# A GRU scan with experts on one core: order of the start's transfers, bias products made once, spare products, and the place of GpSimd's work

## What is computed

```python
def cell(h, x):
    gi = x @ W_ih + b_ih
    gh = h @ W_hh + b_hh
    r = sigmoid(i_r + h_r); z = sigmoid(i_z + h_z)
    n = tanh(i_n + r * h_n)
    return (1 - z) * n + z * h
# for all states h of the scan:
logits = h / max(norm(h), 1e-12) @ router_w      # softmax, the top 2, renormalised
out = x + sum_e combine[:, e] * (h @ Wa[e] @ Wb[e])
```

## Time and profile before

| | |
|---|---|
| median of 3 runs | 1004.74 us (1004.66 to 1004.81) |
| the profiled execution | 1004.69 us |
| its span in the trace | 1002.9 us |
| PE busy | 968.7 us, 97% |
| DVE busy | 881.9 us, 88% |
| ACT busy | 692.6 us, 69% |
| POOL busy | 290.7 us, 29% |
| granted clock of PE, mean | 0.999 |

### The profile page before, as it was taken

How to read it: one execution, slowest core, us unless ns; L and a number is a source line. 1 busy time by engine, 2 the same in 40 slices (tenths; PEclk the granted TensorE clock), 3 DMA queues, 4 the chain that set the end, 5 groups by cost and what they waited for, 6 DMA issues and landing times.

```text
span 1002.9 us, 60804 instructions
## 1 busy us (share of the span) xinstructions
PE 968.7 (97%) x28971; PEld 673.8 (67%) x21187; DVE 881.9 (88%) x3653; ACT 692.6 (69%) x2697; POOL 290.7 (29%) x756
## 2 busy tenths in 40 slices
PE   4689999999999999999999999999999999999997
PEld 2456767677767677767677667777667767667764
DVE  5999888888888888888888888888888888888887
ACT  6776667766766676676676676676677677666664
POOL 1032333232323232223232223232233232233232
PEclk9999999999999999999999999999999999999999
DMA  8600111111111111111011111111111111110001
GB/s 298 176 22 19 30 33 30 28 30 32 29 32 33 25 30 34 27 33 33 25 30 36 26 32 32 26 30 36 27 33 30 28 30 33 30 31 20 14 8 30
DMA packets 50512, 39.10 MB, mean 39 GB/s; under 512 B 35684, under 2 KB 40124, under 8 KB 50236
## 3 DMA queue, kind: packets, MB, share of 16 engines
q1 hardware_dynamic: 49388, 31.67, 12.1%
q10 hardware_dynamic: 848, 3.54, 1.1%
HBM read 18.94 MB, written 8.39 MB: 27 GB/s over the span
## 4 chain that ended last, share of the span: by engine, by line
PE 88%; DVE 7%; ACT 2%; DMA 1%; issue 1%; ACTq 0%; DVEq 0%; POOL 0%; POOLq 0%
PE pairs L923 17%; PE ybank L923 11%; PE gates L1003 11%; PE gates L1008 10%; PE pairs L914 6%; PE ybank L914 5%; PE zbank L923 5%; PE zbank L914 5%; PE tbank L923 3%; PE obank L923 3%; PE nbank L923 3%; PE tbank L914 2%; PE obank L914 2%; PE nbank L914 2%; DMA wih<-in_L_cond_W_ih 1%; DVE tr L779 1%
## 5 line engine op out<-in xcount | busy, mean ns | idle before, releaser
L923 PE MATMUL pairs<-wx,xs 128*32 128x384 f16 x4464 | 296.3, 327 | 0.4 <-DVE wx L759 0.4
L643 ACT ACTIVATE rr<-pre 128x64 f32<-128x64 f32 x256 | 65.7, 257 | 235.5 <-DVE pre L782 235.3
L923 PEld LDWEIGHTS pairs<-wx,xs 128*32 128x32 f16 x4464 | 118.5, 97 | 113.0 <-issue 77.2
L923 PE MATMUL ybank<-hparts,wa 128*128 128x128 f16 x2016 | 185.2, 219 | 0.0
L914 PE MATMUL ybank<-hparts,wa 128*128 128x128 f16 x1008 | 173.8, 219 | 0.0
L923 PEld LDWEIGHTS ybank<-hparts,wa 128*128 128x128 f16 x2016 | 156.8, 98 | 23.4 <-issue 10.5
L1003 PE MATMUL gates<-whh,st 128*32 128x256 f16 x4080 | 157.1, 273 | 14.8 <-DVE st L808 14.4
L1008 PE MATMUL gates<-whh,hparts 128*32 128x256 f16 x4080 | 157.3, 273 | 0.0
L1003 PEld LDWEIGHTS gates<-whh,st 128*32 128x32 f16 x4080 | 105.2, 96 | 62.0 <-ACT gates L615 34.2
L923 PE MATMUL zbank<-whh,hparts 128*32 128x128 f16 x4080 | 145.5, 219 | 0.0
L914 PE MATMUL zbank<-whh,hparts 128*32 128x128 f16 x4080 | 145.5, 219 | 0.0
(11 more groups left out here) (153 smaller groups left out, 1891.6 us busy)
## 6 DMA issues: line engine op xcount, KB each, us to landing
out<-outb SPq DMA_DIRECT2D x63, 128.0 KB
xin<-in_x SPq DMA_DIRECT2D x60, 128.0 KB
wih<-in_L_cond_W_ih ACTq DMA_DIRECT2D x4, 768.0 KB, 7.5
whh<-in_L_cond_W_hh SPq DMA_DIRECT2D x4, 768.0 KB, 12.0
wih<-in_L_ffn_Wb SPq DMA_DIRECT2D x8, 256.0 KB, 5.2
xs<-xh SPq DMA_TRANSPOSE x120, 3.2
wih<-in_L_ffn_Wa SPq DMA_DIRECT2D x4, 256.0 KB, 6.0
whh<-in_L_ffn_Wa SPq DMA_DIRECT2D x4, 256.0 KB, 4.5
```

What stands on the lines that cost most here:

```text
L643: nc.scalar.activation(rr[:, :], pre[:, RG, :, :].rearrange("p k b -> p (k b)"), ACT.Sigmoid, scale=1 / PROD_SCALE).then_inc(r_ready, 1)
L923: return nc.tensor.matmul(out, lhsT, rhs, start=start, stop=stop, skip_group_check=True)
```

## The change

- SP's queue gets W_ih 0 and 1, `cond`, W_ih 2 and 3, W_hh 0, x block 0, W_hh 1 to 3, x block 1, the router's weights; x block 2 goes between the first loads of the experts' weights. ACT's queue gets the biases only.
- The bias products go into the first bank of `pairs` only; the second is begun with zero products, and ACT copies the first into it (`keep_biases`).
- `turn_first(1)` moves behind step 0 on PE, its high part to step 0 on ACT and its low part to step 1 on DVE; `split_x(FIRST)` on ACT moves from step 0 to step 1. In ACT's and DVE's lists before step 0, block 0, the kept biases and the seeds change their places.
- 16 spare products stand on PE ahead of block 0, 4 behind step 0. Their results aren't used.
- POOL: in steps up to 17 (`QUIET`) its work of a step, except norm, logits, gaps and `combine`, waits for the gate products of the next step. In all steps `gaps` comes before `low_y`, and both `less_upper_half` stand at s = 1.
- `LOW_AT` moves late pieces of DVE between steps.

```diff
+    QUIET = 2 * S + 1
-    LOW_AT = {1: 3, 2: 2, 3: 3, 4: 3, 5: 2, 6: 3, 7: 2, 8: 2, 9: 2, 10: 2, 11: 2, 12: 1, 14: 2, 15: 2, 17: 2}
+    LOW_AT = {1: 1, 2: 2, 3: 3, 4: 3, 5: 2, 6: 3, 7: 2, 8: 2, 9: 3, 10: 2, 11: 1, 12: 2, 13: 1, 14: 2, 15: 2, 17: 2}
+    WARM = 16
+    FILL = 4
...
+            load_ih(0)
+            load_ih(1)
+            load_cond()
+            load_ih(2)
+            load_ih(3)
+            load_hh(0)
+            load_first(0)
+            for k in range(1, K):
                 load_hh(k)
+            load_first(1)
             sp.dma_start(rw32[:, :, :], router_w.rearrange("(p k) e -> p k e", k=K)).then_inc(rw_loaded, 16)
-            sp.wait_ge(whh_loaded[1], 16)
-            load_first(1)
-            sp.wait_ge(whh_loaded[2], 16)
-            for half in range(2):
-                load_x(FIRST, half)
             sp.wait_ge(weights_split, splits_before(N_IH_SPLITS))
             for i in range(LEAD):
                 load_late(i)
+                if i < 2:
+                    load_x(FIRST, i)
...
             def beside(n):
                 i, s = n // S, n % S
+                if s == 3 and 1 <= i:
+                    invert_norm(i - 1)
+                    sum_logits(i - 1)
+                    gaps(i - 1)
+                if s == 4 and 1 <= i:
+                    combine(i - 1)
+
+                if n <= QUIET:
+                    pool.wait_ge(rh_done, n + 2)
                 if s == 0 and 1 <= i:
                     fold_squares(i - 1)
                     add_squares(i - 1)
-                if s in (1, 2) and 1 <= i:
-                    less_upper_half(i - 1, s - 1)
-                if s == 3 and 1 <= i:
-                    invert_norm(i - 1)
-                    sum_logits(i - 1)
-                if s == 4 and 1 <= i:
-                    combine(i - 1)
+                if s == 1 and 1 <= i:
+                    for part in range(2):
+                        less_upper_half(i - 1, part)
                 if s in (5, 6) and i + 2 < NB:
                     split_x(i + 2, s - 5, n)
                 for m in reads_at(n):
                     low_y(m)
-                if s == 3 and 1 <= i:
-                    gaps(i - 1)
...
             def keep_biases():
                 act.wait_ge(bias_done, 1)
-                nc.scalar.activation(bias_sums[:, :], pairs[1][:, P:4 * P], ACT.Copy).then_inc(bias_kept, 1)
+                nc.scalar.activation(bias_sums[:, :], pairs[0][:, P:4 * P], ACT.Copy).then_inc(bias_kept, 1)
+                nc.scalar.activation(pairs[1][:, :], pairs[0][:, :], ACT.Copy).then_inc(bias_kept, 1)
...
             for n in range(N_GRU_SPLITS):
                 split_weights(n)
-                if n == 8:
-                    split_first(0)
-                if n == N_IH_SPLITS:
+                if n == N_IH_SPLITS - 1:
                     keep_biases()
+                if n == N_IH_SPLITS + 2:
                     copy_high(-1)
                     act.wait_ge(consts_ready, N_CONST)
-                if n == N_IH_SPLITS + 3:
+                    split_first(0)
+                if n == N_IH_SPLITS + 8:
                     seed(0)
                     seed_z(0)
-            split_first(1)
...
+            def spare_products(count):
+                for _ in range(count):
+                    nc.tensor.matmul(nbank[:, 0:3 * P], wx[:, 0, 0, 0, 0:P], wx[:, 0, 0, 0, :], start=True, stop=True,
                                      skip_group_check=True)
...
+            put_first_biases()
+            pe.wait_ge(hi_split, 3)
+            spare_products(WARM)
             pe.wait_ge(ident_step, 2)
             turn_first(0)
-            put_first_biases()
             wait_turned(0)
             for k in range(K):
                 first_parts(k)
             pair_part(1, range(6))
-            turn_first(1)
             first_state_part()
             grouped_step(0)
+            spare_products(FILL)
+            turn_first(1)
```

More of the change, by code:

```diff
@@ L491, in less_upper_half @@
                 if f < NB - 1:
-                    pool.wait_ge(both_parts_ready, 2 * ((f + 1) * S + 3 + part))
+                    pool.wait_ge(both_parts_ready, 2 * ((f + 1) * S + 3))
                 nc.gpsimd.tensor_tensor(sqs[:, part + 1, :], sqs[:, part, :], upper_half(part), ALU.subtract
@@ L583, in _, with load_biases @@
         def _(act):
-            for k in range(K):
-                if k == 2:
-                    act.dma_start(xin[:, 0, :], x_blocks[0]).then_inc(first_loaded[0], 16)
-                act.dma_start(wih32[:, k, :, :].rearrange("p g n -> p (g n)"), W_ih[k * P:(k + 1) * P, :]
-                              ).then_inc(wih_loaded[k], 16)
+            groups = "(g j c) -> j g c"
+            def load_biases():
+                act.wait_ge(consts_ready, 2)
+                act.dma_start(bias_h[0:P:32, HN, :], b_hh[2 * D:3 * D].rearrange("(j c) -> j c", j=K)).then_inc(bias_loaded, 16)
+                act.dma_start(bias_h[0:P:32, RG:ZG + 1, :], b_hh[0:2 * D].rearrange(groups, g=2, j=K)).then_inc(bias_loaded, 16)
+                act.dma_start(bias_i[0:P:32, :, :], b_ih.rearrange(groups, g=3, j=K)).then_inc(bias_loaded, 16)
             def split_weights(n):
@@ L711, in beside @@
                 if n == 0:
+                    split_first(1)
+                if n == 1:
                     split_x(FIRST)
@@ L898, in _ @@
                 if n == 8:
+                    turn_state()
+                if n == N_IH_SPLITS + 2:
+                    low_state()
                     split_first(0)
-                if n == 8:
-                    turn_state()
-                if n == N_IH_SPLITS:
-                    low_state()
             turn_n(0, 0)
@@ L961, in put_first_biases @@
                 pe.wait_ge(bias_loaded, 16 * 3)
-                for bank in pairs:
-                    nc.tensor.matmul(bank[:, 0:4 * P], spread_rows[:, :],
-                                     bias_h[:, :, :].rearrange("p g c -> p (g c)"), start=True, stop=False,
+                nc.tensor.matmul(pairs[0][:, 0:4 * P], spread_rows[:, :], bias_h[:, :, :].rearrange("p g c -> p (g c)"),
+                                 start=True, stop=False, skip_group_check=True)
+                nc.tensor.matmul(pairs[0][:, P:4 * P], spread_rows[:, :], bias_i[:, :, :].rearrange("p g c -> p (g c)"),
+                                 start=False, stop=True, skip_group_check=True).then_inc(bias_done, 1)
+            def spare_products(count):
+                for _ in range(count):
+                    nc.tensor.matmul(nbank[:, 0:3 * P], wx[:, 0, 0, 0, 0:P], wx[:, 0, 0, 0, :], start=True, stop=True,
                                      skip_group_check=True)
-                    mm = nc.tensor.matmul(bank[:, P:4 * P], spread_rows[:, :],
-                                          bias_i[:, :, :].rearrange("p g c -> p (g c)"), start=False, stop=True,
-                                          skip_group_check=True)
-                mm.then_inc(bias_done, 1)
             def first_parts(k):
@@ L1149, in _ @@
             zeros = st[:, :, :].rearrange("p k c -> p (k c)")
-            for g, n_cols in ((gates, 2), (zbank, 1)):
+            for g, n_cols in ((gates, 2), (zbank, 1), (pairs[1], 4)):
                 for c in range(n_cols):
```

27 lines of the change are left out of this document (14 added, 13 removed).

## The result

The changed kernel takes 1008.72 us (median of seven executions), against 1004.97 for the kernel before on the same chips (1004.66 to 1005.73): ratio 1.0035, 95% interval 1.0022 to 1.0047. One of the seven took 1668.69 us at a granted clock of 0.558 and counts as disturbed; the other six lie at 1007.95 to 1009.23, with 1008.59 as their median. The kernel is slower by 3.6 to 3.8 us. The profiled execution took 1007.95 us, 3.3 more than before's 1004.69, and is the fastest of the six, so its trace shows the start of a good execution and not of a typical one.

A forecast was written before the change was run, and what follows sets the result against it. PE, busy throughout, and a loop of dependent operations with 0.1 us of slack per step were taken to bound the kernel. 1004.74 - 2.3 (start) + 1.0 (steps 1 to 17) + 4.5 (s = 3) = 1007.9 us; own range 1005.3 to 1010.2.

The forecast's parts named there:

- s = 3: Every eighth step: `gaps` first puts POOL's two y's among the loop's last DVE operations; 0.15 per period, +4.5 us.
- The start: Up to step 0: W_ih first on SP's queue brings DVE's last split to 23.6 from 25.9 us; -2.3 us.
- the landing of the last W_hh: In the start: weights at 419 GB/s and block 0 at 1.4 us put it at 20.1 to 20.9 us.
- Close to the path but not on it: In the start: block 0 lands at about 15.5, is split by 17.5 and multiplied by 19.6, when the seeds are next.
- Spare products cost nothing: On PE: 16 stand before block 0 lands, where PE idles; four behind step 0 cost 0, at most 0.4.
- Steps 1 to 17: Late splits and the gate on rh_done together: +1.0 us, range -1.5 to +2.
- the late pieces: DVE's splits moved between steps: step 9 +0.06, steps 12 and 13 +0.33 each, step 11 -0.09; sum +0.6.
- the gate: Steps up to 17: waiting on rh_done moves POOL's meetings with DVE onto L782; 2.8 us for 2.4 now.
- The folds: POOL's two folds, 0.74 and 0.46, cost the chain about 0.42, at steps 8 and 16.
- A: Rival: the y's miss the loop at s = 3; 1003.4 us (10%), or 1000.9 if the gate frees DVE (12%).
- B: Rival: the start gains nothing, the rest as forecast; 1010.2 to 1010.5 us, 8%.
- C: Rival: only the start's gain comes, steps 1 to 17 and the eighth steps unchanged; 1002.4 us, 10%.

The follow-up runs named there:

- the edit alone: The kernel before with only `gaps` moved ahead of `low_y` at s = 3: 1010.23 us, ratio 1.0055.
- the meeting taken away: The changed kernel with `gaps` put back behind `low_y` at s = 3: 1003.65 us, ratio 0.9988.
- the y's behind the next state: The changed kernel, `gaps` still first, with the two y's of s = 3 moved to the next step behind its low half: 1003.72 us, ratio 0.9982.
- the replanned kernel: The kernel with `gaps` behind `low_y`, plus two early splits on ACT, late pieces spread anew, gate ending at step 15, router's weights ahead of block 1: 1002.96 us.

## Why the prediction was right, and where it wasn't

Forecast 1007.9, measured 1008.72; the sign and the main mechanism held. Term by term, against the profile:

- **s = 3, forecast +4.5 (range 0 to 6): +5.14, and +5.3 by the edit alone.** The reading was right in place and kind: y's behind the picks, in the loop, two late operations, 30 times. It came as the variant that the prediction names: L799 (`npre`) slips in first, the first y falls on L802 (`v`), whose delay the wait for tanh hides, and the second on L804 (`u`), which is paid. 0.17 per period instead of 0.15. The page SBUF — State Buffer of the Trainium skill (Who interferes with whom) has the holder keep the shared pair for its whole instruction; `v` and `u` ending 0.14 and 0.09 us behind the two y's agree with it. The forecast by that page, 30 x 0.17 = 5.1, had the right size by luck: it was for a y ahead of L799, which didn't happen.
- **The start, forecast -2.3 (range -3.3 to -0.5): -1.61 in the profile.** In the other kernels with this start state 0 came at 26.73 to 27.32 us where the clock stayed full, -1.8 to -1.2, and at 27.72 to 28.00 where it fell. The median of the changed kernel seems to hold both kinds: three of its executions have a mean granted clock of 0.999 or 1.000 and take 1007.95 to 1008.46 us, three have 0.997 or 0.998 and take 1008.72 to 1009.23. So the start brought less there than in the profile. The term that was mis-sized is the landing of the last W_hh: forecast at 20.1 to 20.9 us, it comes at 21.72, by the trace's record of landings, 0.46 later than in the kernel before (21.26). I let weights flow at 419 GB/s throughout and block 0 cost 1.4 us. The stretches show

```profile
9.00:12.00 3.00, 3.00 (x7) 1.14 (x6) 2.93 (x6) 2.52 (x5) 0.00 (x0) 1.00 1.02 418
12.00:15.00 3.00, 3.00 (x15) 1.59 (x13) 2.74 (x6) 3.00 (x7) 1.08 (x2) 1.00 1.06 257
15.00:18.00 3.00, 0.93 (x6) 0.42 (x4) 1.87 (x4) 1.30 (x4) 0.00 (x0) 1.00 1.00 381
```

  257 GB/s where block 0 is among them and 381 behind it. By the landings, W_hh 0 to W_hh 1, with block 0 between, takes 4.23 us (13.45 to 17.68) where W_hh 2 alone takes 1.89: block 0 costs about 2.3, the difference, and not 1.4. DVE's wait before block 0 is 1.13 us where I had allowed 1.2 for all gaps together; three of 0.26 to 0.28, one before each part of W_hh that it had to wait for, come on top. And ACT, which has the seeds from 21.17 to 21.86 ahead of the last W_hh, starts on it at 21.78, so the seeds and the landing hold it up to the same moment. From there to DVE's last split it is 2.55 us, as forecast (0.6 + 1.90). The page DMA: Bandwidth & Descriptors of the Trainium skill (Specifications) has about 358 GB/s as the limit for one core; it was exceeded here too (418 and 381), so the row was the better guide. No run has the new order of transfers and nothing else.
- **"Close to the path but not on it", of block 0: on it at full clock already, by the seeds, and plainly when the clock is low.** Where the first pair's products ran at half rate, the seeds waited for them, and ACT's split of the last W_hh for the seeds: ACT started on it 0.5 us after its landing with POOL's order as before, 1.8 us without spare products, and state 0 came at 27.7 to 28.9 instead of 26.9. The prediction had no term for the clock.
- **"Spare products cost nothing": true, but that was half of it.** I costed what they take and never asked what would be lost without them. Taken out, they cost 2.0 us of start in the profiles (0.8 us by the ratios, whose intervals overlap); without them this start brought nothing in its profile (28.90 against 28.51). So what the start gained hangs on them, for a reason that the forecast didn't name. That the clock's level causes it is read from the durations at either level, not shown by a run in which only the clock changed.
- **Steps 1 to 17, forecast +1.0: +0.78, by the wrong split.** I gave +0.6 to the late pieces and +0.4 to the gate. The late pieces alone make +0.79; the new order of POOL, gate and all, makes nothing in the sum. In the trial of the pieces alone steps 12 and 13 take +0.34 and +0.25, as forecast (+0.33 each), but step 9 takes +0.50 where I had +0.06, since the third piece lies beside POOL's work, and step 11 gives 0.30 back where I had 0.09. With the gate, step 9 is +0.33, near the 0.06 + 0.25 of the forecast. The folds cost step 16 0.38, as the "about 0.42" had it. L802 was to be lengthened to 0.4 in steps 6, 7, 9 and 17; it takes 0.42 to 0.67 in steps 5, 8, 9, 10, 16 and 17, and 0.26 and 0.22 in steps 6 and 7. Two of these meetings, at steps 5 and 8:

```profile
46.72 0.45 DVE L799 STREAM_TRANSPOSE tr<-gates 128x256 f32<-128x256 f32 x1
47.20 0.67 DVE L802 TENSOR_TENSOR pre<-tr 128x64 f32<-128x64 f32 x1
...
58.67 0.42 DVE L802 TENSOR_TENSOR pre<-tr 128x64 f32<-128x64 f32 x1
```

  L802 is lengthened as foreseen, at step 8 by 0.2. At step 5 it is lengthened by 0.44 where I gave xh 0.16, because POOL didn't begin with the transpose:

```profile
47.12 0.67 POOL L485 TENSOR_TENSOR xh<-x,xh 128x256 f16<-128x256 f32 x1 [33.67 <-PE gates L1028]
50.85 0.68 POOL L485 TENSOR_TENSOR xh<-x,xh 128x256 f16<-128x256 f32 x1 [3.06 <-PE gates L1028]
```

  The first starts 0.40 behind the transpose, which waits for the same products. At step 6, the second starts 0.03 ahead of the transpose (at 50.88). Step 5 therefore gained nothing (4.09 against 4.05), step 6 0.46 (3.73 against 4.19).
- **At nothing:** the bias products, zero products, ACT's extra copy, the four spare products and the turning of block 1 behind step 0: state 0 to 1 takes 3.64 us, before 3.65. The SP queue's wait: no sign of it. Both held, also `less_upper_half` at s = 1, as far as the steps show.
- **Not forecast:** -0.91 at s = 6, and +0.21 in the tail, which I had called unchanged (last section).

Sum: -1.6 + 0.8 + 5.1 - 0.9 - 0.2 + 0.2 = +3.4, forecast +3.2. Part of that nearness is luck: the start brought 0.7 less than forecast and the loop cost 0.6 more, and 1.1 that wasn't forecast came back in other steps. By the medians the difference is 3.6 to 3.8. Of the rivals, A had the right price for the rest: with the meeting taken away the kernel takes 1003.65, forecast 1003.4. B fell in the profile (-1.61), C by the 30 steps at s = 3.

## What to carry to other kernels

Where a loop of dependent small operations sets the rate, an engine that is idle 70% of the time isn't free to use: ask of each of its operations in which part of the loop it will now lie, and whether an operation there is lengthened by it and has no wait to hide that in; moving two operations of 0.43 us to about 2 us later in the step cost 0.5% of the run. Cost a spare or warming instruction from both sides, what it takes and what would be lost without it, and look at a matmul's duration, not only at busy columns. When work is moved between steps, add up each step's free place (here 0.86 us) before and after; the three steps that got pieces too many (9, 12 and 13) grew by 1.1 us together, and planning the list by the measured prices brought 0.7 us.

## What the runs showed of the hardware that was not expected

- PE's granted clock can fall again in the start, after 7 to 10 us at the full one: to 0.50 (1.2 GHz) in five of the thirteen profiles (for example from 19.5 to 22.9 us with POOL's order as before, and from 18.2 to 21.6 with the y's behind the next state). Two of the five are of kernels with before's start. PE has idle times of 1.5 us and more between its bursts there, and the same instructions kept 1.00 in other profiles. In the three profiles of a new start in which it fell, PE was idle for 1.5 to 2.2 us between the 16 spare products and block 0, and the clock had risen at 11.4 to 13.1 us; in the four with the changed kernel's spare products and W_ih first on SP's queue that kept 1.00, PE was idle for 0.6 to 1.1 us there and the clock had risen at 13.8 to 14.0. With seven more spare products behind block 0 the clock stayed, with 2.0 us idle ahead of it. That the idle time causes the fall isn't shown. As for the price, of the replanned kernel's eleven executions the eight with a mean granted clock of 0.999 or 1.000 take 1002.58 to 1003.22 us, the three with 0.998 take 1003.96 and 1003.97; of the kernel with the y's behind the next state, four with 0.999 take 1002.71 to 1003.07 and seven with 0.998 take 1003.61 to 1004.44. So a lower mean clock goes with about 1 us.
- POOL doesn't start at a fixed time behind its release. At the step of the earlier trace rows in the kernel before, the first y's input is ready at 264.24 and POOL starts at 264.69; in the changed kernel ready at 264.45, start at 264.61:

```profile
264.18 0.27 ACT L711 ACTIVATE y<-ybank 128x128 f32<-128x128 f32 x1
...
264.61 1.20 POOL L510 TENSOR_TENSOR y<-y 128x128 f16<-128x128 f32 x3
...
265.81 0.21 DVE L812 TENSOR_TENSOR pre<-tr 128x64 f32<-128x64 f32 x1
```

  0.45 us against 0.16. By that the third y misses L812 (the old L792, 0.46 in the earlier trace rows). Four steps of the kernel before (n = 62, 86, 110, 134) are lengthened so, 3.99 to 4.17 us; in all kernels with the new start they take 3.81 to 3.83. This is the -0.91 at s = 6. It isn't a gain of the new start: in the replanned kernel, and in the one with more spare products, four other steps (n = 158, 182, 206, 230) take 3.97 to 4.02 us, and the -0.91 shrinks to -0.16. What decides between 0.16 and 0.45 is open; the start at 47.12 above was late too, by 0.40.
- The tail, from the last state to the end, takes 17.54 us where ACT's queue carries only the biases, and 17.35 with W_ih on it too (17.33 before). DVE's last operations and the last packets of `out` (16.52 us behind the last state) stand at the same distance from it in both kernels; later is only SP's closing semaphore event, the last of the trace (17.53 us behind the last state, against 17.28 before). The cause is open.
